# Gated attention in a four-layer decoder: two heads as row tiles of 64 partitions, one PSUM bank per head, keys without zeroed halves

## The reference, cut to what matters

```python
def expert_step(acc, params):
    qw, qb_, kw, kb_, vw, vb_, ow, ob_, g = params
    q = (x @ qw.T + qb_).reshape(B, S, H, Dh).transpose(0, 2, 1, 3)
    k = (x @ kw.T + kb_).reshape(B, S, H, Dh).transpose(0, 2, 1, 3)
    v = (x @ vw.T + vb_).reshape(B, S, H, Dh).transpose(0, 2, 1, 3)
    scores = jnp.einsum('bhqd,bhkd->bhqk', q, k) * scale
    p = jax.nn.softmax(scores, axis=-1)
    o = jnp.einsum('bhqk,bhkd->bhqd', p, v)
    o = o.transpose(0, 2, 1, 3).reshape(B, S, E) @ ow.T + ob_
    return (acc + o * g[..., None], None)
```

## Time and profile before

| | |
|---|---|
| Time, median of 3 executions | 3807.44 us (3804.05 to 3823.59) |
| Profiled execution, its own time | 3820.63 us |
| Its span | 3818.7 us |
| Mean granted clock of TensorE | 0.853 |
| TensorE, matmul busy | 75% |
| VectorE, ScalarE, GpSimd busy | 53%, 36%, 17% |
| DMA | 57 GB/s over the span |

### The profile page before, as it was taken

How to read it: one execution, slowest core, us unless ns; L and a number is a source line. 1 busy time by engine, 2 the same in 40 slices (tenths; PEclk the granted TensorE clock), 3 DMA queues, 4 the chain that set the end, 5 groups by cost and what they waited for, 6 DMA issues and landing times. The chain is left out here.

```text
span 3818.7 us, 62592 instructions
## 1 busy us (share of the span) xinstructions
PE 2878.4 (75%) x23570; PEld 2120.4 (56%) x23570; DVE 2028.2 (53%) x6834; ACT 1361.3 (36%) x3026; POOL 639.8 (17%) x853
## 2 busy tenths in 40 slices
PE   5887867665777877878878878878878878959453
PEld 2344646533565755746746746746646646738352
DVE  3566344466444356656656556556656566554411
ACT  1333323232554733323323324324334333327210
POOL 1122111233211011111111111111111111110303
PEclk8778989876988988978979979979879889879776
DMA  6201535300544500000000000000000000014353
GB/s 231 100 23 49 175 120 173 103 25 23 179 145 146 156 9 7 2 8 7 2 8 7 2 9 5 3 8 5 4 10 2 4 9 2 2 36 128 96 144 102
DMA packets 146506, 216.98 MB, mean 57 GB/s; under 512 B 20376, under 2 KB 99232, under 8 KB 146080
## 3 DMA queue, kind: packets, MB, share of 16 engines
q1 hardware_dynamic: 133920, 187.79, 16.2%
q0 software_dynamic: 12288, 25.19, 2.3%
HBM read 159.82 MB, written 53.08 MB: 56 GB/s over the span
## 5 line engine op out<-in xcount | busy, mean ns | idle before, releaser
L1099 ACT ACTIVATE ex<-bank 128x512 f32<-128x512 f32 x896 | 483.3, 601 | 675.6 <-PE bank L441 453.1
L1531 DVE TENSOR_REDUCE mx<-bank 128x4 bf16<-128x512 f32 x640 | 406.7, 684 | 82.8 <-PE bank L422 44.4
L927 POOL TENSOR_TENSOR rstd<-vare,power 128x2 f32<-128x2 f32 x192 | 138.6, 722 | 1378.9 <-DVE vare L1350 1378.4
L936 POOL DMA_INDIRECT sent<-tail_tok,pos x192 | 192.4, 1002 | 601.2 <-DVE pos L1472 557.9
L368 PE MATMUL bank<-hT,wproj 128*128 128x256 f32 x736 | 275.2, 477 | 12.5 <-ACT hT L1069 12.2
L991 POOL TENSOR_TENSOR oT<-oT 128x128 f32<-128x128 f32 x256 | 118.5, 463 | 952.3 <-DVE oT L1644 952.2
L524 PE MATMUL bank<-qm,expert 128*128 128x128 f32 x1872 | 273.4, 293 | 2.0 <-ACT ex L1099 1.4
L596 PE MATMUL bank<-ev,ex 128*128 128x65 f32 x2048 | 271.4, 277 | 0.0
L596 PEld LDWEIGHTS bank<-ev,ex 128*128 128x128 f32 x2048 | 263.9, 196 | 6.1
L524 PEld LDWEIGHTS bank<-qm,expert 128*128 128x128 f32 x1872 | 252.5, 209 | 6.4 <-issue 6.2
L358 PE MATMUL bank<-ident,h_tok 128*128 128x128 f32 x224 | 69.0, 406 | 233.1 <-DVE h_tok L1361 124.7
(11 more groups left out here) (200 smaller groups left out, 5376.4 us busy)
## 6 DMA issues: line engine op xcount, KB each, us to landing
expert<-in_moe SPq DMA_DIRECT2D x78, 578.0 KB, 4.0
expert<-in_moe SPq DMA_DIRECT2D x78, 512.0 KB, 3.8
expert<-in_moe SPq DMA_DIRECT2D x78, 384.0 KB, 3.3
sent<-zeros SPq DMA_DIRECT2D x8, 2560.0 KB, 8.6
qm<-sent SPq DMA_DIRECT2D x234, 64.0 KB, 3.6
answered<-qm SPq DMA_DIRECT2D x234, 64.0 KB, 3.4
ctxT<-ctx_kept SPq DMA_DIRECT2D x32, 128.0 KB, 2.1
wproj<-in_wproj SPq DMA_DIRECT2D x1, 3328.0 KB
```

The source lines that it names most:

```text
L936: nc.gpsimd.indirect_dma_start(sent[s][:], bass.IndirectOffsetOnAxis(ap=pos[s][:, i, j:j + 1], axis=0), tail_tok[s][:, j // 2, :], None).t ...
L1099: give(nc.scalar.activation(ex[s][:, i], ps[:].rearrange("p (i q) -> p i q", i=4), ACT.Exp, scale=SCALE), *key)
L1531: give(nc.vector.tensor_reduce(mx[s][:, b, HB * i:HB * i + HB], ps[:].rearrange("p (i k) -> p i k", i=HB), AX.X, ALU.max), *k, "s", b, i)
```

## The change

The two heads of a pair are no longer separated by zeros but by partitions. `ek` holds each key once. `scores(p)` and `scores_t(p)` work on a head pair and both sequences: head `i` multiplies over its own 64 partitions, as a row tile, into a bank of its own, and matmuls of the two heads alternate. So scores are eight matmuls of 128 columns with eight weights (before, four of 256 with four), and `scores_t` four of 256 columns over 64 partitions (before, four of 256 over 128). Each fills two banks at once, "s1" or "s2" whole. The maxima and exponentials are per head with both sequences in a bank, and as many as before. A head pair has two steps instead of two units: step A has the scores, the next keys and `scores_t`, step B the next queries, `weigh` for both sequences, values and the turn; there are 11 of each. The keys are one activation of 128 partitions, and six memsets fall away. The diff, cut to its core:

```diff
-        ek = [two(f"ek{i}_", [P, 2, NT]) for i in range(3)]
+        ek = [two(f"ek{i}_", [P, NT]) for i in range(3)]
...
-                    def scores(u):
-                        p, b = u // NB, u % NB
-                        ps = open_bank("s1", *k, "s", u)
-                        if b == 0:
-                            taken(*k, f"k{p}")
-                            taken(*k, f"q{p}")
+                    def head(i):
+                        return slice(HE * i, HE * (i + 1))
+                    def scores(p):
+                        taken(*k, f"k{p}")
+                        taken(*k, f"q{p}")
+                        ps = [open_bank("s1", *k, "s", p, i) for i in range(2)]
+                        for b in range(NB):
+                            for j in range(2):
+                                for i in range(2):
+                                    c = 2 * b + j
+                                    mm = nc.tensor.matmul(ps[i][:, c * P:(c + 1) * P],
+                                                          eq_bf16[s][p % 3][head(i), j, seq(b)],
+                                                          ek_bf16[s][p % 3][head(i), seq(b)], start=True, stop=True)
+                                    if c == 2 * NB - 1:
+                                        filled(mm, *k, "s", p, i)
+                    def scores_t(p):
+                        ps = [open_bank("s2", *k, "sT", p, i) for i in range(2)]
+                        for b in range(NB):
+                            for i in range(2):
+                                nc.tensor.matmul(ps[i][:, 2 * b * P:2 * (b + 1) * P], ek[p % 3][s][head(i), seq(b)],
+                                                 eq[s][p % 3][head(i), :, seq(b)], start=b == 0, stop=False)
                         for i in range(2):
-                            mm = nc.tensor.matmul(ps[:, 2 * i * P:2 * (i + 1) * P], eq_bf16[s][p % 3][:, i, seq(b)],
-                                                  ek_bf16[s][p % 3][:, :, seq(b)], start=True, stop=True)
-                        filled(mm, *k, "s", u)
-
-                    def scores_t(u):
-                        p, b = u // NB, u % NB
-                        ps = open_bank("s2", *k, "sT", u)
-                        out_ = ps[:].rearrange("p (s i q) -> p s i q", s=2, i=2)
+                            taken(*k, "s", p, i)
+                            for c in range(2 * NB):
+                                mm = nc.tensor.matmul(ps[i][:, c * P:(c + 1) * P],
+                                                      emax[s][:, 2 * (p % 2) + i, c:c + 1].to_broadcast([P, P]),
+                                                      identb[:, 1, :], start=False, stop=c == 2 * NB - 1)
+                            filled(mm, *k, "sT", p, i)
+                    def weigh(p):
+                        taken(*k, f"v{p}")
                         for i in range(2):
-                            nc.tensor.matmul(out_[:, :, i, :], ek[p % 3][s][:, i, seq(b)], eq[s][p % 3][:, :, seq(b)],
-                                             start=i == 0, stop=False)
-                        taken(*k, "s", u)
-                        for i in range(4):
-                            mm = nc.tensor.matmul(ps[:, i * P:(i + 1) * P],
-                                                  emax[s][:, u % 4, i:i + 1].to_broadcast([P, P]),
-                                                  identb[:, 1, :], start=False, stop=i == 3)
-                        filled(mm, *k, "sT", u)
-
-                    def weigh(u):
-                        p, b = u // NB, u % NB
-                        ps = open_bank("g", *k, "o", u)
-                        if b == 0:
-                            taken(*k, f"v{p}")
-                        taken(*k, "sT", u)
-                        for i in range(4):
-                            mm = nc.tensor.matmul(ps[:, i * (HE + 1):(i + 1) * (HE + 1)],
-                                                  ex[s][:, u % 4, i, :], ev[s][:, p % 2, b, i % 2, :],
-                                                  start=True, stop=True)
-                        filled(mm, *k, "o", u)
+                            taken(*k, "sT", p, i)
+                        for b in range(NB):
+                            ps = open_bank("g", *k, "o", p, b)
+                            for c in range(4):
+                                j, i = c // 2, c % 2
+                                mm = nc.tensor.matmul(ps[:, c * (HE + 1):(c + 1) * (HE + 1)],
+                                                      ex[s][:, 2 * (p % 2) + i, 2 * b + j, :], ev[s][:, p % 2, b, i, :],
+                                                      start=True, stop=True)
+                            filled(mm, *k, "o", p, b)
...
-                    for n in range(EUNITS + 4):
-                        if n < EUNITS:
+                    for n in range(HP + 3):
+                        if n < HP:
                             scores(n)
-                            if n % NB == 0 and 3 <= n // NB + 1 < HP:
-                                keys(n // NB + 1)
-                        if 1 <= n <= EUNITS:
+                        if 3 <= n + 1 < HP:
+                            keys(n + 1)
+                        if 1 <= n <= HP:
                             scores_t(n - 1)
-                        if n % NB == 0 and 2 <= n // NB + 1 < HP:
-                            queries(n // NB + 1)
-                        if 2 <= n <= EUNITS + 1:
+                        yield "gated unit", 2.7 if 1 <= n < HP else 1.8 if n == HP else 0.5, 0.3
+                        if 2 <= n + 1 < HP:
+                            queries(n + 1)
+                        if 2 <= n <= HP + 1:
                             weigh(n - 2)
-                        if n % NB == 0 and 2 <= n // NB < HP:
-                            values(n // NB)
-                        if n % NB == 1 and n >= 5:
-                            turn_mixed((n - 5) // NB)
-                        if n == 0:
-                            yield "gated unit", 0.25, 0.9
-                        elif n <= EUNITS:
-                            yield "gated unit", 2.4 if n % 2 else 3.5, 0.0
-                        else:
-                            yield "gated unit", 0.9, 1.0
+                        if 2 <= n < HP:
+                            values(n)
+                        if n >= 3:
+                            turn_mixed(n - 3)
+                        yield "gated unit", 3.6 if 2 <= n < HP else 2.5 if n <= HP + 1 else 0.3, 0.3 if n <= HP else 1.5
...
-                for i in range(3):
-                    pool.memset(ek[i][s][:], 0.0).then_inc(sem["consts_set"], 1)
...
-                        for i in range(2):
-                            r = slice(HE * i, HE * (i + 1))
-                            ins = nc.scalar.activation(ek[p % 3][s][r, i, :], ps[r, 0:NT], ACT.Identity,
-                                                       bias=col(f"Ek{p}")[r])
+                        ins = shifted(ek[p % 3][s][:], ps[:, 0:NT], f"Ek{p}")
...
+                        if 1 <= n <= HP:
+                            p = n - 1
+                            for i in range(2):
+                                exp(2 * (p % 2) + i, (*k, "o", p - 2, NB - 1) if p >= 2 else None, *k, "sT", p, i)
+                        yield "gated unit"
...
+                    def maxima(p):
+                        for i in range(2):
+                            ps = take(*k, "s", p, i)
+                            give(nc.vector.tensor_reduce(emax[s][:, 2 * (p % 2) + i, :],
+                                                         ps[:].rearrange("p (c k) -> p c k", c=4), AX.X, ALU.max),
+                                 *k, "s", p, i)
...
+                        if n < HP:
+                            maxima(n)
+                        yield "gated unit"
+                        if 2 <= n + 1 < HP:
+                            queries(n + 1)
+                        for b in range(NB if 2 <= n < HP + 2 else 0):
+                            weighted_sums(n - 2, b)
                         yield "gated unit"
```

71 lines of the change are left out of this document (29 added, 42 removed).

## The result

The changed kernel takes 3851.95 us (median of 5 runs, 3847.71 to 3858.09), the kernel before beside it 3808.95 (5 runs). The ratio is 1.0106, 95% interval 1.0082 to 1.0130: **slower by 1.1%**. The prediction was 3774, faster. What was missed is how much the granted clock depends on which wait stands where. The profiled executions took 3858.09 and 3820.63 us, so what is read from profiles adds up to a difference of 38 us, where the medians give 43.

The account below looks back on a forecast made before the run. In gated stretches TensorE's own instruction order was the limit (90% and 89% busy). -79 + 10 + 10 + 15 + 10 = -34 us from the profiled 3820.63 gave 3787; from the median 3807.44, 3774; range 3722 to 3840, forecast's own 3725 to 3788.

Parts of the forecast that it names:

- The tiles' price and gain: Gated `scores_t` and `scores` as row tiles cost 1.18 and 0.45 us a pair; gain 0.56 a pair, 79 us in all.
- Rivals 3 and 4: Two tiles of 64 run one after another: 3928 us, chance 0.06; tiling without a price: 3697 us, chance 0.07.
- The four terms: Losses against the gain: banks 0 to 3, 10 us; ring "g", 10; other stream's chains, 15; end of gated attention, 10.
- the 15 for h_tok: Other stream's VectorE chains, filled by the pairs: longer waits for h_tok and some half clock, 1.9 us a period, 15 us.
- the place of ring "g": Attention's scores behind a full step B wait for VectorE to free both sums' banks: 23 x 0.45 = 10 us.
- a net 10: Attention's `scores_t` behind step A waits for exponentials in banks 2 and 3: 24 us, less 14, net 10 us.
- The end of a gated attention: Leftover steps and turns, with `out` behind the next stream's first scores: 0.6 us per gated attention, 10 us loss.
- half clock in one place: A longer wait for h_tok may put the following unit's `scores_t` at half clock: 0.84 us.
- signs of being wrong: L585's group above 1.7 us; TensorE idle above 12 us in gated stretches; longer stops lowering their clock, 0.97 and 0.88.
- Rival 2: Each step A ends in a 1.1 us stop for its second exponential: slower, 3904 us; chance 0.12.
- -26 and -20: Low end of the range: end of a gated attention a gain (-16 for +10), half of the stops (another -20).
- The count of places: Attention's `scores_t` over four banks behind step A 28 times; attention's scores behind a full step B 23 times.

Follow-up runs that it names:

- experiment 14: Changed kernel with the planner's delays of steps A and B at 0 instead of 0.3, another order of the same instructions; ratio 0.9886 to the kernel before.
- Experiment 6: Changed kernel with attention's `scores_t` opening its four banks one by one instead of all ahead of the first matmul; 3814.14 us, ratio 1.0007.
- Experiments 3: Changed kernel with filler, two extra matmuls whose result nothing uses, ahead of each wait for h_tok; 3787.61 us, ratio 0.9950.
- 4: Kernel before with filler, two extra matmuls whose result nothing uses, ahead of each wait for h_tok; 3758.74 us, ratio 0.9883.
- Experiment 13: Kernel before with each unit's `scores_t` filling two banks, one per head, an exponential for each, and no tiles; ratio 1.0118.
- 5: Changed kernel with the planner's delay of the last steps B of a gated attention 0 instead of 1.5; 3877.13 us, ratio 1.0184.
- 18: Changed kernel with the planner's delay of step A at 1.0 instead of 0.3; ratio 1.0105 to the kernel before.
- 12: Kernel before with unused matmuls ahead of waits for h_tok and attention's `scores_t` banks opened one by one; 3754.21 us, ratio 0.9879.
- experiment 7: Kernel before, its units and order kept, with row tiles in gated `scores_t` alone, each head's half in its own bank; 3845.22 us, ratio 1.0092.
- 8: Kernel before with row tiles in gated `scores_t` alone, plus two unused matmuls ahead of each wait for h_tok; 3828.77 us, ratio 1.0053.
- 10: Kernel before with the mixture's tiles in banks of ring "g" instead of "s1" and "s2"; 3815.89 us, ratio 1.0021.
- 1: Changed kernel without tiles: its order and banks, heads separated by zeroed halves over 128 partitions again; 3905.47 us, ratio 1.0254.
- experiments 2: Changed kernel with the products of `scores_t` ahead of `scores` inside step A; 3838.11 us, ratio 1.0086.
- 15: Kernel before with the planner's delay of a gated unit at 0.3 instead of 0; ratio 0.9963.
- 17: Changed kernel with unused matmuls ahead of h_tok waits, attention's `scores_t` banks opened one by one, and `scores_t` products ahead of `scores`; ratio 0.9908.

## Why the prediction was wrong

- **The tiles' price and gain: right**, 1.60 us a pair for 1.63. Work fell by 89 us in the middle, 112 pairs, 0.80 a pair, and by 71 in experiment 14, 0.63; the sum had 0.56. The surplus may come from ways in and out that are paid less often than twice a pair, and from the split. Rivals 3 and 4 are out.
- **The waits' own length: right in sum.** The four terms (10 + 10 + 10 and, of the 15 for h_tok, 8 as waiting) are 38 us of idle time; measured +37 in the middle. That it agrees so well is in part luck. Measured in the middle: h_tok +10 for 8; L415, the place of ring "g", +14 for 10; L430 +21 for a net 10. The end of a gated attention, 10 in the sum, shows no loss: `out` and the turn of the router's weights wait 11 us less. Not in the list are L575's wait, in the main for both maxima (+11), and L367's (+8), and against them the maxima's (-8) and that for tail_tok of VectorE's L1356 (-6).
- **The step that failed is the clock.** The prediction priced half clock in one place, 0.84 us a period, some 7 us, and scaled the gain by 1.10. Measured: +73 us in the middle, so what the tiles saved went back as slower matmuls. Experiment 6 shows the cause at one place: with TensorE at work through the stops ahead of attention's `scores_t`, the clock gives back 38 us while idle time and work together grow by 7. Experiment 14 shows it for the kernel: the same instructions in another order cost 19 us of clock instead of 73 and 1 us of idle time instead of 37, in the middle against the kernel before (its profile is from another chip). Experiments 3 and 4 show that the clock behind waits for h_tok is worth 45 us and more in either kernel, which is little of the difference. What part of the 73 the tiles have (28 us less without them) is open. The prediction said itself that longer stops could take the clock of the gated stretches down, gave no price for it, and left it out of the chances. Of its signs of being wrong, this one came. The other, more than 12 us of idle time in the gated stretches, did not (9.0 and 11.0), though the kernel is slower.
- **The tail, +12 us, was priced at nothing.** Experiment 13 shows that a second bank and exponential can lengthen it, by another wait than the changed kernel has; there it stays open. The head's 5 us are within what executions differ by.
- **Rival 2**, slower by the missing second bank, had the sign and the place, and decided from 57 stops of 1.1 us. There were fewer; by experiment 6 they counted for more than their length.
- **The range's low end is a slip.** Its own terms, -26 and -20 from 3774, give 3728, not 3725 or 3722.
- **The order was taken for given.** The count of places (28 and 23) was made from the planner's order as it stood. Experiment 14, held against 5 and 18, shows that this order decides the sign. What stays open is a rule that says beforehand which order is good: the number of stops behind step A isn't it.

The best kernels measured are the kernel before with filler (experiments 4 and 12, ratios 0.9883 and 0.9879) and the changed kernel with the order of experiment 14 (0.9886); their intervals overlap. Filler on experiment 14's order was not tried.

## What to carry to other kernels

When two streams share one engine's order, time a change with several orders (a planner's delay or two, moved a little) before judging it: here four orders lay 3% apart, and the change's own arithmetic was 2%. Price each new stop twice, once by its length and once by the work behind it that then runs at half clock; here, with a mean clock of 0.85, the second was the larger (73 us for 37). And a saving on TensorE stayed where the stops between its work didn't grow (experiment 14), and was given back where they did.

## What the runs showed of the hardware

- Matmuls that compute nothing made both kernels faster by 45 and 59 us, with the mean clock going from 0.853 to 0.886 (before) and from 0.833 to 0.870 (changed).
- In several kernels the steady periods fall on evenly spaced values: 273.1 (experiments 4 and 12), 276.5 (6), 279.9 (before, 7, 8, 10), 283.3 (13), 286.7 (5) and 290.1 us (1). So 36 us less work over seven periods (experiment 7) changed a steady period by nothing. It is no rule for all: experiments 2, 14, 15 and 17 have periods in between that vary.
- Two row tiles of 64 partitions do overlap: 8 records of 256 columns in 1.07 us, for 1.72 of the same number over 128 partitions, at 0.20 us for the way out of one group and into the next.
- A group of tiled matmuls takes less than twice its time at half clock: L585 1.97 us for 1.07.
